# Another order of ACT's work in the second sweep, and the last tokens' routing at the sweep's end

## The reference

```python
x = x + ffn(cond(x, ids))                # x: 8 x 256 x 1024, float32
# cond: base = x W^T; logits = x Wr^T, plus 5 on the language's expert; top 2 of 8 experts,
#       softmax -> gates; h = x A_e^T (rank 16); out = base + 2 * sum_e gate_e * (h_e B_e^T)
# ffn:  dots = softmax(y centroids^T / 0.1)      # 64 clusters
#       hits = dots > 0.01
#       row of tokens kept if any cluster hits; column kept if its cluster was hit by any token
#       out = where(kept row & kept column, y weight^T + bias, 0)
```

## Time and profile before

| | |
|---|---|
| median of 3 runs | 376.43 us (374.96 to 377.31) |
| profiled execution: time, span | 375.24 us, 373.1 us |
| PE busy | 347.7 us, 93% |
| PEld busy | 304.7 us, 82% |
| DVE busy | 253.2 us, 68% |
| ACT busy | 133.7 us, 36% |
| transfers | 49.10 MB, mean 132 GB/s |
| granted clock of TensorE, mean | 0.975 |

### The profile page before, as it was taken

How to read it: one execution, slowest core, us unless ns; L and a number is a source line. 1 busy time by engine, 2 the same in 40 slices (tenths; PEclk the granted TensorE clock), 3 DMA queues, 4 the chain that set the end, 5 groups by cost and what they waited for, 6 DMA issues and landing times.

```text
span 373.1 us, 4828 instructions
## 1 busy us (share of the span) xinstructions
PE 347.7 (93%) x1892; PEld 304.7 (82%) x1892; DVE 253.2 (68%) x439; ACT 133.7 (36%) x215; POOL 1.0 (0%) x9
## 2 busy tenths in 40 slices
PE   7899999998969897896997899999999999999993
PEld 6788889998969887896985588888888888888882
DVE  2627878456656647656766788985949598594936
ACT  4544563244433351454335142233213223321210
POOL 1000000000000000000000000000000000000000
PEclk9999999999987998998899999999999999999999
DMA  7667331433331332321380315272542707251202
GB/s 281 240 232 254 112 124 57 171 112 114 114 112 56 114 113 87 115 83 56 114 325 13 115 56 193 90 259 78 181 159 83 251 5 257 80 184 42 84 30 112
DMA packets 13782, 49.10 MB, mean 132 GB/s; under 512 B 1664, under 2 KB 1664, under 8 KB 13760
## 3 DMA queue, kind: packets, MB, share of 16 engines
q1 hardware_dynamic: 13760, 48.80, 36.3%
HBM read 40.41 MB, written 8.39 MB: 131 GB/s over the span
## 4 chain that ended last, share of the span: by engine, by line
PE 80%; DVE 9%; ACT 5%; DMA 4%; issue 1%; SPq 1%; DVEq 0%
PE ps L926 27%; PE ps L928 26%; PE ps L927 26%; DVE gop_lo L581 3%; DMA xt_raw<-in_xt 2%; DVE xt_lo L581 2%; DMA vt_raw<-in_v 2%; ACT gop_hi_t L393 1%; DVE hgt_lo L581 1%; ACT gop_hi_r L393 1%; ACT hgt_all L393 1%; ACT hgt_hi L393 0%; SPq L297 0%; PE ps L986 0%; ACT gb_hi L393 0%
## 5 line engine op out<-in xcount | busy, mean ns | idle before, releaser
L926 PE MATMUL ps<-vt_hi,w_hi 128*128 128x288 f32 (+1 forms) x216 | 71.5, 331 | 2.0 <-DVE vt_lo L581 2.0
L927 PE MATMUL ps<-vt_lo,w_hi 128*128 128x288 f32 (+1 forms) x216 | 70.5, 327 | 0.0
L928 PE MATMUL ps<-vt_hi,w_lo 128*128 128x288 f32 (+1 forms) x216 | 70.4, 326 | 0.0
L927 PE MATMUL ps<-gop_lo,sl_s_hi 128*128 128x512 f32 x128 | 49.8, 389 | 0.0
L393 ACT ACTIVATE u<-ps 128x512 f32<-128x512 f32 x32 | 19.1, 598 | 83.9 <-PE ps L928 54.2
L926 PEld LDWEIGHTS ps<-vt_hi,w_hi 128*128 128x128 f32 x216 | 40.8, 189 | 5.5 <-DVE vt_lo L581 1.6
L927 PEld LDWEIGHTS ps<-vt_lo,w_hi 128*128 128x128 f32 x216 | 40.7, 189 | 2.8
L928 PEld LDWEIGHTS ps<-vt_hi,w_lo 128*128 128x128 f32 x216 | 40.6, 188 | 2.9
L926 PE MATMUL ps<-aw_hi,xt_hi 128*128 128x200 f32 x128 | 38.6, 301 | 0.1
L927 PE MATMUL ps<-aw_lo,xt_hi 128*128 128x200 f32 x128 | 38.2, 298 | 0.0
L928 PE MATMUL ps<-aw_hi,xt_lo 128*128 128x200 f32 x128 | 38.0, 297 | 0.0
(11 more groups left out here) (123 smaller groups left out, 640.9 us busy)
## 6 DMA issues: line engine op xcount, KB each, us to landing
xt_raw<-in_xt SPq DMA_DIRECT2D x32, 512.0 KB, 3.7
nat<-in_x SPq DMA_DIRECT2D x16, 512.0 KB, 4.3
out<-nat SPq DMA_DIRECT2D x15, 512.0 KB, 2.7
wraw<-in_w SPq DMA_DIRECT2D x9, 512.0 KB, 3.3
w_raw<-in_w SPq DMA_DIRECT2D x8, 512.0 KB, 3.1
vt_raw<-in_v SPq DMA_DIRECT2D x4, 576.0 KB, 4.3
vt_raw<-in_v SPq DMA_DIRECT2D x4, 512.0 KB, 6.3
awt_raw<-in_awt SPq DMA_DIRECT2D x1, 544.0 KB, 6.1
```

The costliest lines, as they stand in the source:

```text
L926: nc.tensor.matmul(dst, l_hi, r_hi, start=start, stop=False, skip_group_check=True)
L927: nc.tensor.matmul(dst, l_hi, r_lo, start=False, stop=False, skip_group_check=True)
L928: return nc.tensor.matmul(dst, l_lo, r_hi, start=False, stop=stop, skip_group_check=True)
```

## The change

On ACT, in each step of the second sweep, the rounding of G's pieces (`r_part`, `t_part`) moves from behind `keep_hgt` to a place right behind `split_x(0, n)`, ahead of `router_exp`; the rounding of the next block of W (`split_w`) moves from ahead of `split_x(1, n)` to behind `keep_hgt`. No instruction is added or removed.

At the end of the sweep, the last pair's chain moves. On PE `turn_hg(7)` stands right behind `chunk(KD, 1)` instead of within iteration 0, and `lora_logits(7)` ahead of the S2 product instead of behind the S1 product. On DVE `route(7)` stands behind `rest_a(0)` instead of behind `rest_s(0)`; `split_hgt(7)`, `softmax_max(7)` and `softmax_hits(7)` come earlier, the latter two with the counting of hits ahead of `rest_a(1)`. ACT's `router_exp(7)`, `keep_hgt(7)` and `softmax_exp(7)` move to match.

```diff
             for n in range(NPAIR):
                 if n >= 1:
                     split_x(0, n)
+                    if n >= 2 and n % 2 == 0:
+                        r_part(n // 2 - 1, slice(A1, HALF), chunk_number(n - 1, 1))
+                    elif n >= 2:
+                        t_part(n // 2 - 1)
                     router_exp(n - 1)
                 evict(n, 0)
                 if n >= 1:
-                    split_w(n + KG + 1)
                     split_x(1, n)
                     keep_hgt(n - 1)
-                if n >= 2 and n % 2 == 0:
-                    r_part(n // 2 - 1, slice(A1, HALF), chunk_number(n - 1, 1))
-                elif n >= 2:
-                    t_part(n // 2 - 1)
+                    split_w(n + KG + 1)
                 evict(n, 1)
                 if n >= 1:
                     softmax_exp(n - 1)
...
             t_part(KH - 1)
+            router_exp(NPAIR - 1)
             evict(KD, 0)
             hi_hgm(0)
             evict(KD, 1)
+            keep_hgt(NPAIR - 1)
             hi_22(0)
...
-                if i + 1 < NPAIR:
-                    hi_a(i + 1)
-                if i == 0:
-                    router_exp(NPAIR - 1)
+                if i == 0:
                     act.wait_ge(gbd_made, 1)
                     copy(gb3_hi[:], gb3_raw[:]).then_inc(gb3_hi_done, 1)
+                    hi_a(1)
+                    softmax_exp(NPAIR - 1)
                 elif i + 1 < NPAIR:
+                    hi_a(i + 1)
                     hi_22(i + 1)
...
-                if i == 0:
-                    keep_hgt(NPAIR - 1)
...
-                    softmax_exp(NPAIR - 1)
...
             rest_a(0)
+            route(NPAIR - 1)
             s_sums(0)
             t_rest(KH - 1)
             rest_22(0)
             rest_s(0)
-            route(NPAIR - 1)
+            split_hgt(NPAIR - 1)
...
-            split_hgt(NPAIR - 1)
+            softmax_max(NPAIR - 1)
             s_sums(1)
             add11(0)
-            rest_a(1)
-            softmax_max(NPAIR - 1)
-            rest_22(1)
             softmax_hits(NPAIR - 1)
             dve.wait_ge(soft, SOFT_STEPS * NPAIR)
             nc.vector.tensor_copy(hit_b[:], hit_sum[:]).then_inc(hit_ready, 1)
+            rest_a(1)
+            rest_22(1)
...
             chunk(KD, 1)
+            turn_hg(NPAIR - 1)
...
                 if i >= 1:
                     lora21(i)
+                if i == 0:
+                    lora_logits(NPAIR - 1)
                 pe.wait_ge(ss_split, i + 1)
...
-                if i == 0:
-                    turn_hg(NPAIR - 1)
...
                     lora21(0)
-                    lora_logits(NPAIR - 1)
```

## The result

| | before | after |
|---|---|---|
| median | 375.87 us (374.96 to 377.31, 4 runs) | 349.12 us (348.82 to 350.19, 4 runs) |
| ratio, 95% interval | | 0.929 (0.9252 to 0.9328) |
| profiled execution: time, span | 375.24, 373.1 us | 350.19, 348.1 us |

The kernel is 26.8 us faster; 349.5 was forecast, in a range of 348 to 357. In the changed kernel's lines numbers from DVE's part on are one lower than before (L580 for L581, L925 to L927 for L926 to L928).

What follows compares the result with a forecast made beforehand. PE bounds the kernel nearly everywhere; its idle time and the resulting lower clock can be won. Span 373.1 - 21.8 (sweep) - 4.0 (end) = 347.3 us, plus 2.1 around it: 349.5 us, range 348 to 357.

Steps and rivals of the forecast that it cites:

- a clean step: Step 1 of the second sweep before the change, without a wait of PE: 12.59 us; six would take 75.54 us.
- the excess: Second sweep, steps 2 to 7: 21.78 us over six clean steps, 12.5 idle and 9.3 at lower clock, all to go.
- the rival with the kept clock: Second sweep: small matmuls' mix, not idle time, lowers PE's clock; only 12.5 us go, 9.3 stay; 358.8 us, 8%.
- That the moved rounding costs nothing: ACT, second sweep: `t_part` fits 1.95 us of idle time ahead of e, delaying e by at most 0.1 us.
- S: Start of a step of the second sweep; 96.70 us for step 3 in the trace before.
- Slack at hgt_lo: Second sweep: DVE finishes hgt_lo before PE's `lora_logits` by 2.1 us in odd steps, 1.6 in even; all six waits go.
- T: Start of `chunk(KD, 0)` at the end of the second sweep; 180.16 us before the change.
- the three waits of iteration 0: PE's waits for hit_b, hg and gb_lo, 1.4, 1.3 and 0.7 us, go; end-of-sweep gain 4.0 us in total.
- The floor: Whole kernel: PE's busy time, 347.7 us, would allow 349.8 us at best; the slow stretches put the real floor lower.
- Part staying: Sweep's end or even steps: waits return under another name or 1 us stays per even step; some 4 us, 353.5, 15%.
- Waits that move: Second sweep: late `r_part` or `t_part` on ACT holds e, `route` and PE's transpose; 39 us lost, 388 us, 4%.
- The scatter: Run-to-run spread of the kernel before: clock dips of differing depth are a likely cause, and they go; no size given.

Runs made afterwards that it cites:

- R's pieces late: Changed kernel with the rounding of R's pieces (`r_part`) back behind `keep_hgt` in the even steps, T's pieces still early; 352.98 us.
- the additions: Changed kernel with idle 128x256 additions on DVE ahead of hgt_lo: two (349.62 us) or six (357.64) every step; eight (357.31) or eleven (365.69) in steps 3, 5, 7.
- six additions: Changed kernel with six idle additions of 128x256 on DVE ahead of hgt_lo in every step of the second sweep; 357.64 us in one run.
- DVE's late subtraction: Changed kernel with ACT's sweep order as before the change, and DVE's subtraction of G's pieces moved behind hgt_lo; 351.25 us.
- the end alone: Kernel before with all of the change but ACT's new order in the second sweep; 371.08 us, ratio 0.9898.
- W last: Changed kernel with the rounding of G's pieces back behind `keep_hgt` and W's rounding behind that; 370.50 us, ratio 0.9867.

## Why the prediction was right

**What bounds the kernel.** PE, by its waits and by the clock behind them, with a clean step as the measure. The six steps came out at 75.56 us against 75.54 worked out; the excess of 21.78 us went whole. Alone, the sweep's order gave 21.8 us. One split was wrong: of the 9.3 us of the excess that are no idle time the prediction gave all to the lower clock. Steps 2, 4 and 6 last 13.86, 13.85 and 13.86 us, 1.27 us more than a clean step for a wait of 1.00, and with R's pieces late the same 1.27 us stand there at a clock of 1.00. So 0.8 of the 9.3 us are not the clock's, and 8.5 at most are. The total doesn't depend on it, but the rival with the kept clock should have stood at 358.0 and not 358.8.

**That the moved rounding costs nothing.** It started at 95.89, S - 0.47 (0.3 before S was said), and e followed at 97.94, S + 1.58, where it had stood at S + 1.67: not late at all. hg was there at S + 3.4.

**Slack at hgt_lo.** 2.1 and 1.6 us were said for odd and even steps; step 3 shows 1.9 and step 4 1.55 (hgt_lo done at 116.67, the logits at 118.22), and the additions bear the size out. That W's place costs nothing held too. It also gains nothing, and the prediction's remark that the W rounding adds to the queue was wrong: ACT was idle for 0.57 us behind it.

**The end.** 4.0 us were forecast, 3.9 measured alone; in the two traces the stretch from `chunk(KD, 0)` to iteration 1 went from 34.43 to 30.22 us, 4.2 us. The one new wait, PE for the last hg, was put at 0.1 us and is not there: in the trace after, hg ends on DVE at T + 6.2 and PE comes at T + 6.4 (165.71 less 159.33). Iteration 0 was put at 24.0 us with the transposes, which now stand ahead of it; from transpose to iteration 1 it is 23.84.

DVE at the end of the sweep, the answer to the earlier trace rows (T = 159.33):

```profile
159.10 1.81 DVE L583 TENSOR_TENSOR gop_raw<-gop_raw 128x288 f32<-128x288 f32 x4
...
165.15 0.42 DVE L710 TENSOR_TENSOR hg<-ps,gates 128x256 f32<-128x256 f32 x1
...
168.02 2.29 DVE L580 TENSOR_TENSOR gop_lo<-gop_raw,gop_hi_t 128x2048 fp32r<-128x2048 f32 x1
...
173.03 0.42 DVE L580 TENSOR_TENSOR hgt_lo<-hgt_all,hgt_hi 128x256 fp32r<-128x256 f32 x1
...
175.60 1.76 DVE L580 TENSOR_TENSOR gb_lo<-gb_raw,gb_hi 128x1536 fp32r<-128x1536 f32 x1 [1.22 <-ACT gb_hi L393]
...
182.96 0.23 DVE L853 CAST hit_b<-hit_sum 128x128 bf16<-128x128 f32 x1
```

hgt_lo ends at T + 14.1 (14.4 said), gb_lo at T + 18.0 (19.4 at the latest), hit_b at T + 23.9 (24.5 at the latest). Every link came somewhat earlier than its estimate.

**Its account of hit_b** was too simple. It listed the three waits of iteration 0 together and gave the cause of one, e's place on ACT. The runs showed two causes: e for hg and gb_lo, and for hit_b two subtractions ahead of the softmax on DVE. The sum was right since the change moves both.

**The time.** The median, 349.12 us, lies 0.4 us below the forecast. The profiled execution lies 0.7 us above it, and its first sweep alone is 0.93 us longer than the one that the sum started from. Both differences are smaller than the scatter of either kernel, so it is in part luck that the total came out this close; the parts, 21.8 and 4.0 us, don't rest on it.

**The floor.** The Trainium skill, page "Trainium Kernel Development and Optimization", section "Performance Expectations", calls matmul busy time a bad measure of what is left. Here the span after, 348.1 us, is within 0.4 us of the busy time before, 347.7, and the best of the other three executions has a span of 346.7: the old busy time was no floor.

**The rivals.** Part staying: no wait is left in the stretch. The clock falling by itself: fallen, also by experiment, and with it the swing that the Trainium skill, page "TensorE: Matmul & The Clock Gate", section "A second HAM failure mode: psum-queue depth-cycling", describes; this kernel changes banks between its groups and stays at 1.00 for the whole sweep. Waits that move: e came on time. **The scatter** did shrink, from 2.35 to 1.37 us between the extremes of four runs; but the kernel with W's rounding back in its place, whose trace has no dips either, spread over 3.2 us. Only one execution of each kernel has a trace, so the dips are not shown to be the cause. One part of it is seen: the end of the first sweep, which moves by 1.9 us from trace to trace.

## What to carry to other kernels

On engines that work in order, look at what stands behind a wait as well as at what it waits for: here 5 us of ACT's lateness were harmless in themselves, and cost PE 12.5 us of waits because two subtractions that could run stood behind the one that could not. Either cure works, an earlier producer in idle time of its engine or a later consumer; take a clean step from the same trace as the measure, since it holds what the list of waits leaves out, the clock's part above all (the waits are 12.5 of the 21.8 us here). Then move one instruction at a time: by these runs two moves on ACT and DVE at the end and one in the sweep would have done, though these three alone were not run together.

## What the runs showed of the hardware

The length of a wait does not alone decide whether the clock falls behind it. In the sweep it did not fall behind waits of 1.0 and 1.2 us (R's pieces late; six additions), nor behind one of 1.8 us (the last hg in the kernel with DVE's late subtraction, clock 1.00 from there on). It fell behind two of three waits of 1.4 us, equal in length and place in the step, and behind each of three waits of 2.8 us and of the long ones of 3.15 us before.

Outside the sweep it is as mixed. The waits of 1.4 us for hit_b had no dip behind them in any of the three kernels that have them. In the first sweep waits of 1.9 to 2.4 us for vt_lo had a dip in three traces and none in two. The windows behind hit_b's wait before the change, behind a wait of 1.88 us for vt_lo with the end alone, and behind one of 2.01 us in the changed kernel, columns as above:

```profile
210.16:214.00 3.84, 3.84 (x17) 1.00 0.47 141
```

```profile
7.90:12.00 4.10, 3.94 (x10) 0.58 0.99 405
```

```profile
11.41:16.00 4.59, 4.59 (x20) 1.00 0.15 60
```

What tells the waits with a dip from their equals without one stays open. A dip doesn't start exactly when PE does, either. In windows of 1 us the clock is down already in the last 1.2 us of one wait of 3.15 us (W last), and only 2.1 us behind the first wait of 1.4 us; both times are estimates from the mean clock of the window in which it changes. The price differs as well: beyond the wait of 3.15 us, steps 3, 5 and 7 before the change lost 3.3, 1.9 and 3.3 us.

In the low stretches the granted clock reads 0.50 to 0.54 over whole windows, or 0.58 to 0.73 where a window holds some full clock too, and PE counts as busy all through them. So a loss of this kind shows in no list of waits and in no busy share, only in the clock column and in durations.
